# A message-passing megakernel on one core: the count build's part numbers are packed two to a 16-bit word

## The chip, the core and the metric

The kernel runs on one core of one Trainium2 chip. The metric is device time in microseconds (us) from the start to the end of one execution. The core has a matrix engine (TensorE: PE in the profile, with its weight loads as PEld and its instruction sequencer as PEldq), VectorE (DVE), ScalarE (ACT), GpSimd (POOL), SyncE (SP, which issues most DMAs) and 16 DMA engines.

## The reference

Four graph layers work in turn on 6250 nodes with 256 features each, over 100,000 edges, and each adds its result to the features. Cut to what matters here:

```python
edge_index = jnp.stack([src, dst])
h = jnp.maximum(_layernorm(x, axis=-1), 0.0)
x = x + _L0_gnn_ref(h, ..., edge_index)     # three rounds: agg = segment_sum(h[src], dst) / deg; then dense products
h = jnp.maximum(_layernorm(x, axis=-1), 0.0)
x = x + _L1_gnn_ref(h, ..., edge_index)     # attention over the edges
h = jnp.maximum(_layernorm(x, axis=-1), 0.0)
x = x + _L2_gnn_ref(h, ..., edge_index)     # two rounds: agg = segment_sum(x[col], row)
h = jnp.maximum(_layernorm(x, axis=-1), 0.0)
x = x + _L3_gnn_ref(h, src, dst, edge_type_2, ...)
```

The edges are sorted by `dst`, and low destinations get more edges than high ones. Layers 0 and 2 need sums over all edges of a node. The kernel turns these sums into products with a matrix of edge counts, `adj`, which it builds itself from `src` and `dst` at the start.

## The kernel before

The run has these stages: index preparation (0 to about 98 us), the **count build** (about 98 to 1004 us), then the passes that multiply node features with `adj` (layers 0 and 2, `L1352`), and between and behind them the gathers of layers 1 and 3. The change touches the count build alone.

The count build walks over the edges in 1592 steps (`MEETS`). One step is one chunk of 128 edges met with one block of 8 nodes. Steps are grouped in **turns** of 32 (`BUILD`). The first turn is written out, 47 turns run in a loop, and the last two are written out again; the last of them has 24 steps. A step does the following:

- VectorE makes a one-hot matrix of 128x392 for the step (`hot_columns`, L2309) into one of 16 buffers (`HOT`). For every 8 steps it makes one `hot_key` (L2304). It waits until TensorE is within 16 steps before it overwrites a buffer, in groups of 4 steps.
- TensorE multiplies the two into one of four PSUM banks (L1498). The bank is the step's **part number** modulo 4 (`own = z % RING`). Then it waits until the bank after that has been emptied (`evicted >= z`), and clears that bank with a tiny matmul (`cleared`, L1487). Steps with `s % 4 == 0` wait for VectorE as well (`hot`).
- ScalarE empties a finished bank into `staged` (L1723), and SyncE sends it to `adj` in DRAM (L732). There are 808 of these.

A part is a run of steps that add up in one bank. So the part number either stays the same from one step to the next or grows by one. The 1664 part numbers, one 32-bit word for each step (the last 72 are padding), lie in row 0 of the buffer `g_x` under the name `step_part`. A DMA puts them there before the build. TensorE's sequencer takes them into 16 registers (`zs`), 16 steps at a time (`NOW`), with one register load (L1493, TENSOR_LOAD in the profile) at steps 0 and 16 of a turn.

The part number decides the address of both matmuls of a step. So the sequencer computes two addresses in each step: a modulo, two multiplications and an addition for the first, the same with two more additions for the second. The compiler packs up to six such operations into one sequencer instruction (ISA in the listings below, FUSED_REGOPS in the profile). A step has two of them, and a step with a wait for `hot` a third, short one.

Between the steps, TensorE also carries the dense products of layer 0's first round, for one tile of nodes per turn: two transposes ahead of step 12 (`in_T`, L1193), products ahead of steps 29 and 30 (`in_P2`, L1212 and L1214), and products ahead of steps 1 and 2 of the turn after (`in_P3`, L1221). VectorE has a few instructions for these too.

No table sets the order here; it is the order of the code on each engine.

## Time and profile before

| | |
|---|---|
| median of 3 runs | 7671.14 us (7663.33 to 7676.74) |
| the profiled execution | 7667.53 us, of which 7665.8 us from the first to the last instruction |
| TensorE matmul busy, whole run | 82% |
| VectorE, ScalarE, GpSimd busy | 45%, 22%, 29% |
| count build, 100 to 1004 us | TensorE 725.4 us, VectorE 592.5 us, ScalarE 373.0 us busy of 904 |
| granted TensorE clock in the count build | 0.81 of full speed |

Times inside the profile count from the first instruction. A step's place in its turn is not written in the trace; it follows from the products between the steps (L1193 stands ahead of step 12, L1212 ahead of steps 29 and 30, L1221 ahead of steps 1 and 2).

### The profile page before, as it was taken

What the parts mean: (1) busy time and instruction counts of PE and PEld (TensorE: products, weight loads), DVE (VectorE), ACT (ScalarE), POOL (GpSimd) and SP (SyncE); (2) the same over time, 40 slices, a digit from 0 to 9 for tenths busy, and PEclk for the clock granted to TensorE, in tenths of its full rate; (3) what the DMA queues carried; (4) which work ended last, traced back from release to release, by engine and by line L of the source; (5) the groups of instructions that cost most, each with busy time, mean ns of one, the idle gap of its engine ahead of it and who ended that gap; (6) DMA issues with size and microseconds to landing.
All of it is one profiled execution on the core that took longest, in us unless ns stands there. A gap on an engine that the chain in (4) does not pass through costs nothing.

```text
span 7665.8 us, 108469 instructions
## 1 busy us (share of the span) xinstructions
PE 6321.0 (82%) x29032; PEld 4993.3 (65%) x29033; DVE 3412.8 (45%) x9453; ACT 1651.3 (22%) x4349; POOL 2239.8 (29%) x2541
## 2 busy tenths in 40 slices
PE   5877799999999999766676765999999966777677
PEld 3555477778887777655555554777787755555555
DVE  7766666661111222355555566122233324444443
ACT  1344410000000111111111113132233332222222
POOL 1000010001001111366666652000111116666664
PEclk8887799999999999878877887999999988878887
DMA  4566777788779777533333336988977753333332
GB/s 138 181 228 242 256 284 261 256 299 312 273 277 343 262 257 256 184 83 83 85 82 84 83 90 200 333 291 294 354 249 244 243 181 97 102 100 99 100 100 75
DMA packets 606869, 1525.79 MB, mean 199 GB/s; under 512 B 72808, under 2 KB 248915, under 8 KB 606612
## 3 DMA queue, kind: packets, MB, share of 16 engines
q1 hardware_dynamic: 472803, 1129.19, 41.8%
q0 software_dynamic: 133824, 393.46, 17.0%
q8 instruction: 143, 2.34, 0.1%
q14 instruction: 99, 0.80, 0.0%
HBM read 1206.47 MB, written 316.80 MB: 199 GB/s over the span
## 4 chain that ended last, share of the span: by engine, by line
PE 59%; DVE 11%; another core or an unknown queue 11%; issue 8%; DMA 6%; DVEq 2%; ACT 2%; SPq 1%; POOL 0%; ACTq 0%; POOLq 0%
PE psum L1352 33%; PE psum L1498 4%; PE psum L1198 4%; PE psum L1646 3%; PE psum L1618 2%; PE psum L1549 2%; DMA slab<-adj 2%; DVE hot_j L2309 2%; DVE acc L2547 2%; DMA g_own<-own_dram 2%; PE psum L1630 1%; PE psum L1537 1%; PE psum L1193 1%; PE psum L1286 1%
## 5 line engine op out<-in xcount | busy, mean ns | idle before, releaser
L1352 PE MATMUL psum<-X,slab 128*128 128x512 f32 x12495 | 3111.2, 402 | 74.9 <-DMA slab<-adj 41.3
L1352 PEld LDWEIGHTS psum<-X,slab 128*128 128x128 f32 x12495 | 2347.7, 191 | 608.5 <-DVE g_x L2374 89.7
L2547 DVE TENSOR_TENSOR acc<-acc,psum 128x264 f32 (+1 forms) x1660 | 702.8, 423 | 1068.8 <-PE psum L1646 353.0
L1498 PE MATMUL psum<-hot_j,hot_key 128*128 128x392 bf16 x1592 | 570.9, 431 | 164.2 <-DVE hot_j L2309 109.4
L1012 POOL DMA_DIRECT2D table<-s_tab x147 | 80.4, 547 | 1910.8 <-DVE s_tab L2065 1910.8
L1537 PE MATMUL psum<-node_tabs,onehot_t 128*128 x1660 | 274.7, 305 | 378.3 <-ACT onehot_t L1822 348.2
L1537 PEld LDWEIGHTS psum<-node_tabs,onehot_t 128*128 128x128 f32 x1660 | 274.0, 248 | 420.6 <-issue 414.3
L1102 POOL DMA_INDIRECT ring<-gat_table,idx_slot x420 | 415.7, 990 | 261.2 <-ACT idx_slot L1817 138.1
L1102 POOL DMA_INDIRECT ring<-rel_table,idx_slot x420 | 412.6, 982 | 250.2 <-ACT idx_slot L1817 137.7
L1723 ACT CAST staged<-psum 128x392 fp32r<-128x392 f32 x808 | 373.0, 489 | 522.3 <-PE psum L1498 497.0
L1498 PEld LDWEIGHTS psum<-hot_j,hot_key 128*128 128x128 bf16 x1592 | 235.7, 148 | 321.7 <-issue 236.2
L2309 DVE TENSOR_SCALAR hot_j<-iota_j,node_tabs 128x392 bf16<-128x392 bf16 x1592 | 411.2, 318 | 73.7 <-PE psum L1498 73.6
L2353 DVE TENSOR_TENSOR node_tabs<-node_tabs,slab 128x896 f32<-128x896 f32 x343 | 374.5, 1092 | 139.2 <-DMA slab<-adj 129.1
L1618 PEld LDWEIGHTS psum<-hT,wbuf 128*128 128x128 f32 x2064 | 383.5, 234 | 48.4 <-ACT hT L1974 2.6
L2065 DVE TENSOR_TENSOR s_tab<-psum,s_tab 128x256 fp32r<-128x256 f32 x196 | 83.1, 424 | 724.3 <-ACT s_tab L1690 724.3
L1618 PE MATMUL psum<-hT,wbuf 128*128 128x128 f32 x2064 | 375.0, 315 | 1.4 <-ACT hT L1974 1.4
L1685 ACT COPY s_hT<-psum 128x256 f32<-128x256 f32 x273 | 101.7, 373 | 1189.5 <-PE psum L1193 1189.5
L1198 PE MATMUL psum<-wbuf,s_hT 128*128 128x256 f32 (+1 forms) x1484 | 336.9, 363 | 0.0
L1487 PE MATMUL psum<-node_tabs 128*128 128x2 bf16 x1593 | 292.7, 184 | 14.2 <-ACT staged L1723 14.0
L1198 PEld LDWEIGHTS psum<-wbuf,s_hT 128*128 128x128 f32 x1484 | 274.9, 190 | 44.4
L1549 PE MATMUL psum<-ring,onehot 128*128 128x264 f32 x840 | 288.9, 481 | 16.7 <-DVE ring L2567 16.7
L1646 PE MATMUL psum<-ring,onehot 128*128 128x256 f32 x840 | 274.0, 420 | 20.6 <-DMA ring<-rel_table,idx_slot 20.3
(426 smaller groups left out, 8124.2 us busy)
## 6 DMA issues: line engine op xcount, KB each, us to landing
slab<-adj SPq DMA_DIRECT2D x383, 1344.0 KB, 6.7
slab<-adj SPq DMA_DIRECT2D x313, 896.0 KB, 6.2
adj<-staged SPq DMA_DIRECT2D x808, 196.0 KB, 1.9
X<-table SPq DMA_DIRECT2D x32, 1792.0 KB, 13.4
table<-s_tab POOLq DMA_DIRECT2D x196, 256.0 KB, 3.5
g_own<-own_dram POOLq DMA_DIRECT2D x35, 896.0 KB, 8.1
own_dram<-s_out POOLq DMA_DIRECT2D x196, 128.0 KB, 5.1
acc<-zero_rows SPq DMA_DIRECT2D x2, 6600.0 KB, 27.4
```

The source lines that it names most:

```text
L1102: nc.gpsimd.indirect_dma_start(out=to, out_offset=None, in_=tab, in_offset=bass.IndirectOffsetOnAxis(ap=idx_slot[:, r * HALF + u:r * HALF ...
L1198: last = nc.tensor.matmul(ps[:, 0:n], s_hT[:, q, :], w(q), start=(q == 0), stop=(q == Q - 1))
L1352: last = nc.tensor.matmul(sums_of(j), slab[:, slab_at(c), u, j * P:(j + 1) * P], X[:, x_at(p, d), :], start=(d == 0), stop=(d == KT - 1))
L1498: nc.tensor.matmul(psum[:, bass.ds(own, 1), 0:J].rearrange("p o j -> p (o j)"), hot_key[:, s % KEYS // AT_ONCE, :, s % AT_ONCE], hot_j[:, ...
L1537: last = nc.tensor.matmul(ps_log[:, v, :], onehot_t[:, v, :], dst_tab[:, bass.ds(tiles[v], 1), :].rearrange("p t h -> p (t h)"), start=Tru ...
L1549: nc.tensor.matmul(psum[:, v, 0:GW], onehot[:, r * HALF + v, :], homes[r][:, v, :], start=True, stop=True).then_inc(sem("mm"), 1)
L1618: last = nc.tensor.matmul(psum[:, bank, b * P:(b + 1) * P], wbuf[:, q, at:at + P], hT[:, q, :], start=(q == 0), stop=(q == Q - 1))
L1646: nc.tensor.matmul(psum[:, u % GB, 0:D], onehot[:, u, :], homes[r][:, v, 0:D], start=True, stop=True).then_inc(sem("mm"), 1)
L1723: nc.scalar.copy(staged[:, r, :], psum[:, (r + 1) % RING, 0:J]).then_inc(sem("evicted"), 1)
L2309: V.tensor_scalar(hot_j[:, s % HOT, :], iota_j[:], edge_now[:, s:s + 1], None, op0=ALU.is_equal).then_inc(sem("hot"), 1)
L2353: V.tensor_tensor(slab_sum, slab_sum, of[u], ALU.add).then_inc(sem("slab_summed" if u == SIZES[c] - 1 else "slab_partly"), 1)
L2547: V.tensor_tensor(a, a, psum[:, bank, 0:w], ALU.add).then_inc(sem("summed"), 1)
```

## The change

The part numbers of steps 2k and 2k+1 are added, and the sum is kept as one 16-bit word in a new row `pair_part` of 832 words. VectorE makes the row with one instruction on one partition, just before the build starts. TensorE loads 16 such words once per turn, at step 0, and takes a part number out of a sum with an addition (odd steps) and a floor division by two. The two numbers of a pair are equal or differ by one, so that is exact. TensorE now waits for `pair_part` instead of `step_part` before the build.

```diff
+    PAIRS = SB2 * P // 2
...
+                pair_part = sb("pair_part", [1, PAIRS], I16, scope=late)
...
             def build(t, steps):
                 for s in range(steps):
                     beside(in_stages, t, s)
-                    if s % NOW == 0:
-                        pe.load(zs, step_part[0:1, bass.ds(t * BUILD + s, NOW)])
-                    z = pe.snap(zs[s % NOW], min_val=1, max_val=LEAD + ENDED)
+                    if s == 0:
+                        pe.load(zs, pair_part[0:1, bass.ds(t * NOW, NOW)])
+                    if s % 2 == 0:
+                        both = pe.snap(zs[s // 2])
+                    z = pe.snap((both + s % 2) // 2, min_val=1, max_val=LEAD + ENDED)
                     if s % 4 == 0:
                         pe.wait_ge(*ev("hot", t * BUILD + (s + 4)))
...
-            pe.wait_ge(*ev("step_part", 16))
+            pe.wait_ge(*ev("pair_part", 1))
...
             dve.wait_ge(*ev("step_part", 16))
             dve.wait_ge(*ev("parts_stored", 16 * SB2))
+            of_pair = step_part.rearrange("p (n two) -> p n two", two=2)
+            V.tensor_tensor(pair_part, of_pair[:, :, 0], of_pair[:, :, 1], ALU.add).then_inc(sem("pair_part"), 1)
             V.tensor_copy(iota_k[:], iota_row[:])
```

On TensorE, around step 16 of a turn, the instructions stand like this before. L1494 and L1498 ISA are the address arithmetic ahead of a step's matmul, L1487 ISA that ahead of the clearing matmul:

```order
L1494 ISA
L1498 MATMUL psum<-hot_j,hot_key 128x392
L1487 ISA [waits evicted]
L1487 MATMUL psum<-node_tabs 128x2
L1493 TENSOR_LOAD g_x
L1498 ISA [waits hot]
L1498 MATMUL psum<-hot_j,hot_key 128x392
L1487 ISA [waits evicted]
L1487 MATMUL psum<-node_tabs 128x2
```

After, at the same place (the lines have moved by three to five):

```order
L1503 ISA
L1503 MATMUL psum<-hot_j,hot_key 128x392
L1490 ISA [waits evicted]
L1490 MATMUL psum<-node_tabs 128x2
L1503 ISA [waits hot]
L1503 MATMUL psum<-hot_j,hot_key 128x392
L1490 ISA [waits evicted]
L1490 MATMUL psum<-node_tabs 128x2
```

The load ahead of step 16 is gone, the one ahead of step 0 stays, and the number of arithmetic instructions per step is the same. Inside, the first arithmetic instruction of a step has one operation more: five become six (copy or add, divide, modulo, two multiplications, addition), and in a step with a wait for `hot` four become five.

On VectorE, just before the build, before:

```order
L2247 TENSOR_SCALAR tile_base<-tile_f 128x7 [waits dve_once]
L2331 CAST node_tabs<-iota_row 128x128 [waits table_moves,rec_stored,parts_stored,act_made,dve_once]
L2332 CAST iota_keys<-iota_row 128x1024
L2300 COPY node_tabs<-edge_at 128x16
L2081 TENSOR_SCALAR s_hT<-psum 128x256 [waits tile_P3,tile_T]
```

After:

```order
L2252 TENSOR_SCALAR tile_base<-tile_f 128x7 [waits dve_once]
L2337 TENSOR_TENSOR pair_part<-g_x 1x832 [waits table_moves,rec_stored,parts_stored,act_made,dve_once]
L2338 CAST node_tabs<-iota_row 128x128
L2339 CAST iota_keys<-iota_row 128x1024
L2305 COPY node_tabs<-edge_at 128x16
L2086 TENSOR_SCALAR s_hT<-psum 128x256 [waits tile_P3,tile_T]
```

One instruction is added ahead of all that VectorE does for the first step.

## Rows read from the trace of the kernel before

**Rows 1.** Build: busy us (count) of PE, PEld, DVE, ACT, POOL; granted clock, DMA.
```profile
100.00:1004.00 904.00, 725.40 (x3766) 467.80 (x3765) 592.46 (x2124) 373.03 (x808) 62.28 (x108) 0.81 0.59 213
```
**Rows 2.** Who waited for whom, 100 to 1004 us: total us, times, longest.
```profile
ACT staged L1723 <- PE psum L1498: 497.0, 506, 16.7
...
DVE hot_key L2304 <- PE psum L1498: 229.2, 116, 7.6
PE psum L1498 <- DVE hot_j L2309: 109.4, 65, 3.1
DVE hot_j L2309 <- PE psum L1498: 73.6, 48, 4.6
```
**Rows 3.** Matmuls around step 16 of one turn: start, us, [idle before].
```profile
464.92 0.39 PE L1498 MATMUL psum<-hot_j,hot_key 128*128 128x392 bf16 x1 [2.58 <-DVE hot_j L2309]
...
466.01 0.38 PE L1498 MATMUL psum<-hot_j,hot_key 128*128 128x392 bf16 x1
...
466.47 0.54 PE L1498 MATMUL psum<-hot_j,hot_key 128*128 128x392 bf16 x1
...
468.00 0.55 PE L1498 MATMUL psum<-hot_j,hot_key 128*128 128x392 bf16 x1
```
**Rows 4.** Weight loads of steps 15 and 16 in the same turn.
```profile
461.94 0.14 PEld L1498 LDWEIGHTS psum<-hot_j,hot_key 128*128 128x128 bf16 x1
...
464.92 0.14 PEld L1498 LDWEIGHTS psum<-hot_j,hot_key 128*128 128x128 bf16 x1 [2.70 <-issue]
```
**Rows 5.** Granted clock (PEclk) in the two stretches of rows 3.
```profile
464.90:466.30 1.40, 1.38 (x8) 0.95 (x8) 0.00 (x0) 0.71 (x2) 0.00 (x0) 1.00 0.42 158
466.40:469.70 3.30, 3.23 (x17) 2.21 (x17) 2.95 (x11) 1.70 (x5) 0.00 (x0) 0.50 0.61 227
```
**Rows 6.** L1493's register loads: ns min/median/max; all, then four single ones.
```profile
L1493 PEldq TENSOR_LOAD <-g_x x100: 1102/1840/3278, 98.4 to 999.5; - x100
...
L1493 PEldq TENSOR_LOAD <-g_x x1: 1120/1120/1120, 106.2 to 106.2; - x1
...
L1493 PEldq TENSOR_LOAD <-g_x x1: 2351/2351/2351, 462.3 to 462.3; - x1
...
L1493 PEldq TENSOR_LOAD <-g_x x1: 1617/1617/1617, 471.5 to 471.5; - x1
...
L1493 PEldq TENSOR_LOAD <-g_x x1: 1104/1104/1104, 999.5 to 999.5; - x1
```
**Rows 7.** The first matmul behind the load at step 0 at 471.5, with its idle time.
```profile
473.42 0.39 PE L1498 MATMUL psum<-hot_j,hot_key 128*128 128x392 bf16 x1 [1.01 <-DVE hot_j L2309]
```
**Rows 8.** Sequencer arithmetic of the steps: ns min/median/max.
```profile
L1494 PEldq FUSED_REGOPS  x1570: 47/94/108, 100.2 to 1003.6; - x197
...
L1498 PEldq FUSED_REGOPS  x398: 96/98/108, 99.8 to 1002.3; - x199
...
L1487 PEldq FUSED_REGOPS  x1592: 98/100/124, 100.0 to 1003.7; - x199
```
**Rows 9.** Sequencer arithmetic with a division (layer 1's L1537).
```profile
L1537 PEldq FUSED_REGOPS  x830: 98/137/161, 3187.4 to 4540.2; - x166
...
L1537 PEldq FUSED_REGOPS  x5: 107/137/149, 3850.3 to 3851.2; - x5
```
**Rows 10.** Loads of one word: 16-bit (L641) and 32-bit (L602).
```profile
L641 PEldq TENSOR_LOAD <-left_row x1: 309/309/309, 7621.2 to 7621.2; - x1
...
L602 PEldq TENSOR_LOAD <-half_row x44: 303/336/985, 3185.3 to 4528.5; - x44
```
**Rows 11.** A VectorE sum on one partition.
```profile
L2124 DVE TENSOR_TENSOR bound_row<-last_is,chunk_row x1: 961/961/961, 8.4 to 8.4; 1x782 f32<-1x782 int32 x1
```
**Rows 12.** What starts at the end of the build.
```profile
1004.13 2.78 PE L1352 MATMUL psum<-X,slab 128*128 128x512 f32 x8
...
1004.31 1.09 DVE L2347 TENSOR_TENSOR node_tabs<-slab 128x896 f32<-128x896 f32 x1 [6.39 <-PE psum L1498]
1004.55 1.73 POOL L1002 DMA_INDIRECT X<-table,idx_more  x1 [21.09 <-PE psum L1498]
```

More of the change, by code:

```diff
@@ L87, in build @@
     assert BTURNS == T + 1 and SB2 * P - MEETS + ENDED + MORE < ELSEWHERE
+    PAIRS = SB2 * P // 2
+    assert MEETS % 2 == 0 and BTURNS * NOW <= PAIRS
     KT = PARTS * DG // P
@@ L505, in build @@
                              ("cuts", 1), ("bound_read", 1), ("cuts_read", 1), ("z_rows", 1), ("parts_out", 1), ("marks", 1), ("x_ve", 1), ("more_rows", 1),
-                             ("b_self", 1), ("rows2_f", 2), ("x_rstd", 1), ("chunk_i", 1), ("edge_f", 2), ("turn_row", 1), ("w_att", 2 * Q),
+                             ("b_self", 1), ("rows2_f", 2), ("x_rstd", 1), ("chunk_i", 1), ("pair_part", 1), ("edge_f", 2), ("turn_row", 1), ("w_att", 2 * Q),
                              ("amax", 1), ("gdiag", 1), ("dst_tab", 1), ("zs_clamped", 1), ("bn_ve", 1), ("bn_shift", 1),
```

## The prediction

> **What bounds the kernel now.** The change touches only the count build, so I read that stretch first. By its busy times [rows 1] TensorE has 725 us of 904 and VectorE 592, so neither is full. The view of who waited for whom decides between them [rows 2]. VectorE waited for TensorE's L1498 for 229.2 + 73.6 = 303 us, which with its 592 us of work fills its 904 us. ScalarE waited for TensorE for 497 us. Both run behind TensorE. TensorE's own waits are small, and the largest is put down to VectorE's `hot_j`, 109.4 us. That name is wrong for most of it: in the turn of [rows 3] the idle 2.58 us stands exactly ahead of step 16, where the weight loads show a hole of 2.70 us with "issue" as its end [rows 4], and a register load of 2.35 us fills that hole [the one at 462.3, rows 6]. TensorE's sequencer is loading part numbers, and nothing else can be issued meanwhile.
>
> The second question is what paces a step when there is no load. If it were the array, a step would take longer at half clock. The turn of [rows 3] shows both levels of the clock back to back [rows 5]: the four steps from 464.92 to 466.47 run at full clock (2.4 GHz) and take 1.55 us; the next four, to 468.00, run at 0.50 (1.2 GHz) and take 1.53. So the array doesn't set the pace at either level. The sequencer's two arithmetic instructions do, of 94 to 98 and 100 ns [rows 8], with the issue of two weight loads and matmuls between them. **Each nanosecond added to that arithmetic lies on the path, and each taken from the loads comes off it.** At the build's end the next stage starts at once on TensorE, VectorE and GpSimd [rows 12], two of which had waited for L1498, so the whole rest moves with that end.
>
> **The load that goes.** There are 100 loads of 16 words, 1102 to 3278 ns [rows 6]: 50 at step 0 and 50 at step 16. Those at step 16, picked out by their place, sum to 115.7 us, a mean of 2.31 (the first, at 106.2, took 1120 ns, and the last, at 999.5, took 1104; they are the two shortest). One costs a little more than its own length. In the turn of [rows 4], step 16's weight load comes 2.98 us after step 15's; an ordinary step of the kind that waits for `hot` comes 0.46 after the one before (466.01 to 466.47, [rows 3]). That is 2.52 us lost, against 2.35 of the load itself: some 0.16 more, for the address arithmetic and the gaps. So **-(115.7 + 50 x 0.16) = -124 us**.
>
> The Trainium skill, "Runtime: NRT & Kernel Launch", section "Instruction fetch mechanics", puts a register load at about 200 ns per register, even in bulk. By it 16 registers take 3.2 us and the 50 loads 160 us, and the sum below would be 36 us better. The trace has that only as its longest load, so I don't use it.
>
> **The load that stays.** It now reads 16-bit words. No row shows 16 such words at once. A single 16-bit word took 309 ns, a single 32-bit word 303 at the least and 336 in the median [rows 10], so I take the width as free: 0. Below, if two words came in one access, the load at step 0 would halve. The 50 of them sum to 75.0 us, a mean of 1.5 (the one at 471.5 took 1617 ns, [rows 6]), and the build would win up to 50 x 0.75 = 37 us, since TensorE sits idle behind the one at 471.5 for 1.01 us [rows 7]. Above, 16-bit words could cost 10% more, the distance of L602's median from its minimum: 7 us.
>
> **The arithmetic that comes.** Each of the 1592 steps gets one more operation, a floor division by 2. The nearest rows are layer 1's L1537, where four of five instructions have a division and a modulo among six operations and the fifth has the modulo alone [rows 9]: 107 ns without the division, 137 in the median and 149 at the most within one group; 98 and 161 over all. Against the 94 ns of a step's instruction now [rows 8], 137 is +43; against the 98 of a step with a wait I take 135, +37. So 1194 x 43 + 398 x 37 = 66 us. The lower end is 137 - 107 = 30 ns or 48 us; the upper is 161 - 98 = 63 ns or 100 us. I stay near the median, as part numbers are small (at most some 800). Some of it is hidden: around steps 30, 31 and 1 the sequencer is held up by layer 0's products (L1212, L1214, L1221) and has time. That is three steps in 32: 6 us. **+60 us**.
>
> The second arithmetic instruction of a step (L1487) stays as it is, as does the number of instructions, so no gap between instructions is added.
>
> **Before the build.** VectorE's sum over 1x832 stands ahead of everything that the first step needs. A sum over 1x782 took 961 ns [rows 11]. Nothing covers it: **+1 us**. TensorE's changed wait ends with that instruction, long before `hot`, which it awaited anyway.
>
> **Moved waits.** What is late next once the stall at step 16 is gone? VectorE is 16 steps ahead at best and gets its lead back in TensorE's stalls. Its work is 592 us for 1592 steps, or 11.9 us a turn, and a turn is now 18.1 us long and then some 16.8. So it still has 5 us to spare per turn, and I put its new wait at 0. ScalarE spares more [rows 1, 2].
>
> **Sum:** -124 + 60 + 1 = -63 us. Against the profiled execution of 7667.5 us that is 7604.5; it lies 3.6 below the median of the runs, so the forecast for the median is 7671.1 - 63 = **7608 us**.
>
> **Rivals.**
>
> *Two words per access* (7608 - 37 = 7571 us). It speaks for it that the loaded bytes halve; against it, that one word costs the same at either width [rows 10]. 8%. A part of the same size could come from the clock. It stands at half right behind the stall at step 16 [rows 5], and without the stall layer 0's products at steps 29 and 30 may run at full clock; that is at most some 10 us, and in the range.
>
> *The division is dear* (7642 us). If it costs the 63 ns of the upper end in each step, 100 us are added, less 6 hidden: -124 + 94 + 1 = -29. For it: L1537's 149 to 161. Against it: these divide words much larger than ours. 13%.
>
> *VectorE takes over* (7640 us). With the stall gone VectorE's bunched work (`hot_key` and three to four instructions for layer 0 within 8 steps) makes TensorE wait for `hot` once a turn. Half of the gain would go: -32. For it: VectorE loses the stall in which it catches up. Against it: its 303 us of waiting. 10%.
>
> *The end of the build doesn't matter* (7671 us, no change). If the first pass waited for DMAs whose time doesn't depend on the build, the gain would be lost there. Against it [rows 12]: the engines start within half a microsecond of the last step, and GpSimd had been waiting 21 us for it. 4%.
>
> *Slower* (7722 us). One mechanism: the sequencer divides in a loop whose length goes with the quotient's bits, and a small divisor makes it long. It decides from 124/1592 = 78 ns per step. At 110 ns it adds 175 us against 124: +51. The divisors of L1537 are 64 and more, so division by 2 is not shown by any row; but its numbers are larger, and its longest instruction is 63 ns above its shortest, all told. 4%.
>
> *That the loads are not halved* is excluded by the listing: one load is left per turn, and it has 16 registers as before.
>
> **How the numbers follow.** The forecast has 61%, and the rivals 8, 13, 10, 4 and 4%. A measurement of this kernel can tell about 0.2% (15 us) from no change, so faster means below 7656. The forecast and the first three rivals lie there; I take 3% off them for values beyond their middle. Faster 0.89, same 0.07, slower 0.04. The range reaches to the first rival and past the next two: 7568 to 7652. It leaves out the last two and the tails, some 14%.
>
> **What would show it.** The register loads (now on L1496) should be 50, of 1.1 to 2 us each, all ahead of step 0. The median of the first arithmetic instruction of a step should be 130 to 145 ns. Four steps in a row should take about 1.70 us instead of 1.53 to 1.55, at either clock, and the idle time ahead of step 16 should be gone. The build should end near 1004 - 63 = 941 us, and everything behind it should be as long as before. I am wrong if the arithmetic shows 160 ns or more, if the 50 loads change their length by over a third, if TensorE's waits for `hot_j` don't shrink from 109 us to 30 or less, or if the stretch behind the build gives back what the build gains.

## The result, and the profile after

The changed kernel takes **7815.65 us** (median of 4 runs, 7802.06 to 7820.66), against 7667.24 of before (4 runs, 7658.87 to 7676.74) on the same chip. The ratio is 1.019, with a 95% interval of 1.0172 to 1.0209. The forecast was 7608, between 7568 and 7652. So the change costs 148 us where 63 were to be won.

The profiled execution of the changed kernel has a span of 7800.4 us, that of before 7665.8: +134.6. The build ends where TensorE's first pass begins. That is at 1138.48 us, against 1004.13 before [rows 12]:

```profile
1138.48 2.78 PE L1355 MATMUL psum<-X,slab 128*128 128x512 f32 x11
...
1138.72 1.73 POOL L1005 DMA_INDIRECT X<-table,idx_more  x1 [23.74 <-PE psum L1503]
```

So it ends 134.3 us later, and everything behind it is as long as before. The whole loss lies in the build. Its line of busy times (columns as in [rows 1]) and its waits (as in [rows 2]):

```profile
103.00:1138.00 1035.00, 798.44 (x3762) 477.02 (x3762) 586.77 (x2115) 373.66 (x808) 62.15 (x108) 0.79 0.52 186
```
```profile
PE psum L1503 <- issue: 180.5, 49, 5.7
...
PE psum L1503 <- DVE hot_j L2314: 4.0, 3, 1.9
...
ACT staged L1728 <- PE psum L1503: 619.5, 492, 20.4
...
DVE hot_key L2309 <- PE psum L1503: 348.5, 90, 11.6
```

VectorE's and ScalarE's work has not grown, and both wait longer for TensorE than before. TensorE is busy for 798 us where it was for 725, with as many matmuls; the clock explains that below. TensorE's idle time put down to `hot_j` has gone from 109.4 to 4.0 us, as forecast. In its place stand 49 idle times that end with "issue", 180.5 us in all and up to 5.7 us each. The sequencer's instructions tell what it did in them (ns min/median/max, first and last start):

```profile
L1496 PEldq TENSOR_LOAD <-pair_part x50: 3784/4576/6179, 99.2 to 1122.9; - x50
...
L1503 PEldq FUSED_REGOPS  x1194: 132/141/162, 103.3 to 1137.9; - x199
...
L1490 PEldq FUSED_REGOPS  x1592: 98/100/118, 103.5 to 1138.1; - x199
```

The arithmetic with the division has a median of 141 ns; 137 was forecast. The second instruction of a step stays at 100. But the **50 loads that stay take 4.58 us each** where 1.5 was forecast: 230.2 us in all (my sum over the 50 records) against the 75.0 that the same 50 took before. The 50 dropped at step 16 had taken 115.7. Half as many loads, each of half the bytes, cost 39.5 us more than all 100 did.

One turn shows what such a load does behind itself (start, us, [idle before]); below it are three stretches with the granted clock, the third figure from the end:

```profile
465.34 0.36 PE L1503 MATMUL psum<-hot_j,hot_key 128*128 128x392 bf16 x1
469.58 0.54 PE L1503 MATMUL psum<-hot_j,hot_key 128*128 128x392 bf16 x1 [3.87 <-issue]
469.99 1.20 PE L1224 MATMUL psum<-wbuf,s_hT 128*128 128x256 f32 x2
```
```profile
469.30:470.90 1.60, 1.32 (x4) 0.96 (x5) 0.00 (x0) 0.00 (x0) 0.00 (x0) 0.50 0.00 0
470.90:475.00 4.10, 4.10 (x20) 2.32 (x19) 1.58 (x5) 1.70 (x4) 0.00 (x0) 0.55 0.18 65
475.00:478.00 3.00, 2.82 (x19) 1.87 (x17) 3.00 (x12) 2.03 (x5) 1.08 (x2) 1.00 0.81 300
```

TensorE stands still for 3.87 us ahead of step 0, and then runs at half clock (1.2 GHz) just where layer 0's products L1224 come. These are float matmuls that keep the array busy: in the second stretch, which holds steps 1 to 9, it is busy for all 4.10 us. So here the array sets the pace and the sequencer runs ahead of it. In the median over the turns, step 2's clearing matmul starts 2.1 us behind its sequencer instruction, against 0.85 before (from the records). From 475.00 us on the clock is full again. Over the build the mean of these products goes from 474 to 701 ns (last two figures ahead of the idle time: sum in us, mean in ns), first before, then after:

```profile
L1221 PE MATMUL psum<-wbuf,s_hT 128*128 128x256 f32 x194 | 75.3, 474 | 0.0
```
```profile
L1224 PE MATMUL psum<-wbuf,s_hT 128*128 128x256 f32 x196 | 117.1, 701 | 0.0
```

VectorE's sum of the pairs took 1.01 us (forecast 1).

**The table to which I come back.** The time from one step's second sequencer instruction (L1487 before, L1490 after) to the next one's, worked out from the records and summed over the 50 turns, by the step's place in its turn, in us. Halved, pair32 and so on are the experiments below. The last column is how many turns of 50 were at half clock at step 6. Each row is one profiled execution. Probe turned out to be the same program as base, and the two differ by 7.7 us in the sum and by up to 3.9 in a column, so I don't read smaller differences.

| kernel | 0 | 1-4 | 5-9 | 10-15 | 16 | 17-18 | 19-31 | sum | half at 6 |
|---|---|---|---|---|---|---|---|---|---|
| before | 124.1 | 84.0 | 112.6 | 127.1 | 146.9 | 36.8 | 272.3 | 903.7 | 10 |
| after | 279.8 | 92.5 | 144.8 | 141.5 | 25.1 | 40.5 | 310.4 | 1034.6 | 46 |
| base | 122.5 | 85.3 | 115.3 | 126.9 | 148.2 | 36.7 | 274.7 | 909.6 | 11 |
| probe | 123.2 | 84.8 | 111.4 | 126.8 | 146.4 | 36.7 | 272.7 | 901.9 | 10 |
| halved | 122.1 | 92.6 | 124.8 | 139.1 | 143.4 | 40.7 | 290.4 | 953.2 | 14 |
| pair32 | 124.4 | 95.8 | 135.1 | 139.0 | 25.1 | 40.4 | 312.2 | 872.0 | 19 |
| load32 | 185.9 | 83.8 | 136.8 | 130.1 | 23.7 | 36.9 | 298.8 | 896.1 | 42 |
| load32at12 | 41.5 | 97.7 | 113.1 | 314.3 | 23.1 | 36.7 | 270.9 | 897.2 | 5 |
| load16at8 | 41.5 | 146.1 | 208.1 | 125.0 | 23.8 | 37.6 | 361.9 | 944.1 | 21 |
| pair32at8 | 43.1 | 110.8 | 205.1 | 137.0 | 25.5 | 40.9 | 298.8 | 861.3 | 12 |
| load4 | 70.8 | 162.4 | 175.5 | 156.4 | 63.5 | 36.6 | 349.3 | 1014.6 | 42 |

### The profile page after: what moved, and what is told of

It reads as the page before. It is cut to its first block, busy times and chain, and to the rows that moved or that the text cites. A ratio compares the mean times of both kernels' runs of the same rounds, so it can differ in the third digit from the quotient of the medians.

```text
span 7800.4 us, 108373 instructions
## 1 busy us (share of the span) xinstructions
PE 6397.5 (82%) x29032; PEld 5003.0 (64%) x29033; DVE 3407.3 (44%) x9454; ACT 1651.4 (21%) x4349; POOL 2236.6 (29%) x2541
## 4 chain that ended last, share of the span: by engine, by line
PE 58%; DVE 12%; another core or an unknown queue 11%; issue 9%; DMA 6%; DVEq 2%; ACT 2%; SPq 1%; POOL 0%; ACTq 0%; POOLq 0%
PE psum L1355 32%; PE psum L1503 4%; PE psum L1201 4%; PE psum L1651 3%; PE psum L1554 3%; PE psum L1623 2%; DMA slab<-adj 2%; DVE hot_j L2314 2%; DVE acc L2554 2%; PE psum L1635 2%; DMA g_own<-own_dram 1%; PE psum L1542 1%; PE psum L1224 1%; PE psum L1196 1%
## 5 line engine op out<-in xcount | busy, mean ns | idle before, releaser
L1355 PEld LDWEIGHTS psum<-X,slab 128*128 128x128 f32 x12495 | 2345.1, 190 | 610.0 <-DVE g_x L2381 92.6
L1503 PE MATMUL psum<-hot_j,hot_key 128*128 128x392 bf16 x1592 | 600.2, 420 | 215.3 <-issue 180.7
L1015 POOL DMA_DIRECT2D table<-s_tab x147 | 80.3, 546 | 1903.9 <-DVE s_tab L2070 1903.9
L1105 POOL DMA_INDIRECT ring<-gat_table,idx_slot x420 | 416.0, 990 | 254.9 <-issue 124.4
L1623 PEld LDWEIGHTS psum<-hT,wbuf 128*128 128x128 f32 x2064 | 380.7, 232 | 47.6 <-ACT hT L1979 2.6
L1490 PE MATMUL psum<-node_tabs 128*128 128x2 bf16 x1593 | 285.0, 179 | 22.6 <-ACT staged L1728 22.1
L975 POOL DMA_DIRECT2D table<-s_tab x49 | 27.3, 556 | 962.6 <-DVE s_tab L2070 962.6
```

What stands on the lines that cost most here:

```text
L1105: nc.gpsimd.indirect_dma_start(out=to, out_offset=None, in_=tab, in_offset=bass.IndirectOffsetOnAxis(ap=idx_slot[:, r * HALF + u:r * HALF ...
L1355: last = nc.tensor.matmul(sums_of(j), slab[:, slab_at(c), u, j * P:(j + 1) * P], X[:, x_at(p, d), :], start=(d == 0), stop=(d == KT - 1))
L1490: nc.tensor.matmul(bank_ap, iota_k[:], iota_k[:, 0:2], start=True, stop=True, skip_group_check=True)
L1503: nc.tensor.matmul(psum[:, bass.ds(own, 1), 0:J].rearrange("p o j -> p (o j)"), hot_key[:, s % KEYS // AT_ONCE, :, s % AT_ONCE], hot_j[:, ...
L1623: last = nc.tensor.matmul(psum[:, bank, b * P:(b + 1) * P], wbuf[:, q, at:at + P], hT[:, q, :], start=(q == 0), stop=(q == Q - 1))
```

## The experiments

They ran in five groups, each beside runs of before on its own chip. Before took 7180.21, 7663.48, 7618.84, 7186.94 and 7179.76 us there, so only the distance from before within a group counts. All kernels take a part number through a maximum with 0 in place of a copy (in ScalarE's loop too); `base` is before with that alone.

### Which part costs: the load, its place or the division (first group)

**base**, the yardstick:

```diff
-                    z = pe.snap(zs[s % NOW], min_val=1, max_val=LEAD + ENDED)
+                    z = at_least_0(pe, zs[s % NOW], min_val=1, max_val=LEAD + ENDED)
```

> The kernel before, with the copy of each part number into a fresh register written as max(number, 0) instead of min(number, number), on TensorE and on ScalarE; the number of operations is the same. It is the yardstick of the runs beside it. Every theory: 7667 us, within 0.2%; the 100 loads 1.1 to 3.3 us as before, a step's first arithmetic instruction 94 ns.

7185.94 us, ratio 1.0007 (0.9998 to 1.0016).

**pair32**: the changed kernel with its sums in 32-bit words (in `g_x`'s row, over `step_part`):

```diff
+                pair_row = step_part[:, 0:PAIRS]
...
+            V.tensor_copy(pair_row, pair_part).then_inc(sem("pair_part"), 1)
...
-                        pe.load(zs, pair_part[0:1, bass.ds(t * NOW, NOW)])
+                        pe.load(zs, pair_row[0:1, bass.ds(t * NOW, NOW)])
```

> The changed kernel, but the sums of two part numbers are kept as 32-bit words, in the place in g_x where the part numbers lay (VectorE makes the 16-bit row first, then copies it over, about 1 us more). Theory A (a 16-bit word costs a fetch of its own, about 0.29 us each, while 32-bit words cost 0.07 to 0.15): the 50 loads fall from 4.6 to about 1.5 us each and the time to about 7667 - 124 + 70 + 2 = 7615 us. Theory B (the place of the new row makes its load slow, whatever the width): the same, 7615. Theory C (the load at step 0 is long because VectorE no longer gets its lead back at step 16 and is at work on the same memory): the loads stay near 4.6 us and the time near 7815.

7152.49 us, ratio 0.9959 (0.9945 to 0.9973): 28 us under before.

**pair16gx**: pair32, but the row in `g_x` holds 16-bit words, `pair_row = step_part.bitcast(I16)[:, 0:PAIRS]`. Nothing else differs.

> As the run with 32-bit sums, with the same instructions and the row in the same place in g_x, but the words are 16 bits wide. Theory A (width): loads 4.6 us, time 7815. Theory B (place): loads 1.5 us, time 7615. Theory C (moment): loads 4.6 us, 7815, and then the 32-bit run must show the same.

7323.93 us, ratio 1.0202 (1.0189 to 1.0216). The load rows of pair32, then of pair16gx:

```profile
L1508 PEldq TENSOR_LOAD <-g_x x50: 1102/1377/2936, 90.9 to 952.5; - x50
```
```profile
L1508 PEldq TENSOR_LOAD <-g_x x50: 3787/4571/6269, 91.3 to 1116.0; - x50
```

Same place, same moment, same instructions: the word's width alone makes 3.2 us per load in the median, and 171 us of the time. The loss of the changed kernel is that of its 16-bit loads.

**halved**: before with every part number doubled by VectorE and divided by 2 by the sequencer, all 100 loads kept.

```diff
-                    z = pe.snap(zs[s % NOW], min_val=1, max_val=LEAD + ENDED)
+                    z = pe.snap(at_least_0(pe, zs[s % NOW], min_val=0, max_val=2047) // 2, min_val=1, max_val=LEAD + ENDED)
...
+            V.tensor_tensor(step_part, step_part, step_part, ALU.add).then_inc(sem("pair_part"), 1)
```

> The kernel before with its 100 loads of 16 32-bit words; the numbers are stored doubled and each step halves its own with a floor division. It prices the division alone. The profile of the changed kernel shows a step's first instruction at 141 ns instead of 94 (+47) and four steps at 1.70 instead of 1.55 us (+0.04 per step): 1592 x 0.045 = 72 us, less what is hidden at steps 30 and 31: 7667 + 68 + 1 = 7736 us. If the division were hidden at half clock or behind VectorE: under 7700.

7247.07 us, ratio 1.0092 (1.0077 to 1.0108): 61 us above base in the medians, 49 in the two profiled executions (base's was the slowest of its eleven). The 60 us for the division held.

### Is it the word, the sign or the burst (second and third group)

**pairu16** has the changed kernel's row as unsigned words (`mybir.dt.uint16` for `I16`).

> The changed kernel with its row of sums as unsigned 16-bit words in place of signed ones; nothing else differs. If the price is of the width (H1), the 50 loads keep their median of 4.5 to 4.6 us and the time is the changed kernel's: before + 2.0%, within 0.3%. If it is of the sign (H2: each word must be extended with its sign), the loads fall to 1.1 to 1.9 us and the time to before - 0.4%, as pair32.

7804.00 us, ratio 1.0194 (1.0178 to 1.0209), loads 3788/4563/6340 ns. The sign costs nothing.

**pair16in8** loads the sixteen words in two parts:

```diff
-                    if s == 0:
-                        pe.load(zs, pair_part[0:1, bass.ds(t * NOW, NOW)])
+                    if s % NOW == 0:
+                        pe.load(zs[s // 2:s // 2 + NOW // 2], pair_part[0:1, bass.ds(t * NOW + s // 2, NOW // 2)])
```

> The changed kernel, but its sixteen 16-bit words per turn are loaded as eight at step 0 and eight at step 16. If the dear 16-bit load costs by the word (G1: 4576 ns in the median for 16 is 286 a word, and a single 16-bit word took 309 in before), each of the 100 loads takes 2.2 to 2.5 us, their sum stays near 230 us, and the time is the changed kernel's within 0.3%: before + 2.0%. If a load of 16-bit words has a large fixed part (G2, say over 2 us), 8 words take 3.3 us or more, the sum grows by 100 us or more and the time is before + 3.4% or more. If it is the length of the burst that makes it dear (G3: eight words as cheap as 32-bit ones), they take 0.8 to 1.3 us each, and the time falls to about before - 0.2%.

7830.29 us, ratio 1.0226 (1.021 to 1.0241), between G1 and G2. The shortest load of eight took 1917 ns, half of the shortest of sixteen (3784): the price is by the word. The median of 2.85 us is above half of 4.58, because the load at step 16 stands in a costlier place (a mean of 3.37 us there, 2.46 at step 0); before shows that too (2.31 and 1.50).

**probe** was to time single loads ahead of the first step, with values that nothing used:

> Base with a probe ahead of the first step, where TensorE waits for VectorE: 13 register loads, four times over, whose values are not used. 1, 2, 4, 8 and 16 words of 32 bits; the same of 16 bits (from the same row); 16 words of 16 bits at every second place; 16 bytes; 16 words of 32 bits at every second place. By J1 (a narrow word is an access of its own of 250 to 300 ns, 32-bit words go in a burst): 16-bit words 0.3, 0.6, 1.2, 2.3, 4.6 us, 32-bit ones 0.3, 0.35, 0.5, 0.76, 1.1; 16 bytes 4.6 or more; the 32-bit words at every second place between 1.1 and 4.6. By J2 (the dear part is of the moment, not of the width: the array or the queues are busy at step 0): 16-bit loads of 16 words take under 2 us here. The sum of the probe is 50 to 100 us, which delays the first step by 40 to 100 us, as it starts after the last wait but one of TensorE.

7671.19 us (one run), and its trace holds none of the 52 loads: what nothing uses is not in the program. It is another run of base.

**probe2** uses each load's last register:

```diff
+            for _ in range(4):
+                pe.load(zs[0:1], step_part[0:1, 0:1])
+                pe.reg_alu(seen, zs[0], seen, ALU.max)
...
+                pe.load(zs[0:16], halves[0:1, 0:16])
+                pe.reg_alu(seen, zs[15], seen, ALU.max)
```

> The probe again: in the first one the values of its loads were not used, and its trace holds none of them. Now each load's last register goes into a maximum that the first weight load's address uses (its value is 0 at run time). Expected as before: by J1 (a narrow word is an access of its own) 1, 2, 4, 8, 16 words of 16 bits take 0.3, 0.6, 1.2, 2.3, 4.6 us and of 32 bits 0.3, 0.35, 0.5, 0.76, 1.1; 16 bytes 4.6 or more. The 100 loads of eight 16-bit words in pair16in8 took 2.87 us in the median (1.92 to 5.16), so a fixed part of 1.2 us with 0.21 us a word (J3) is possible too: then 1 word takes 1.4, which L652's single word of 0.31 speaks against; or what is in the way is the traffic of the moment (J2), then 16 words of 16 bits take under 2.5 us here.

7704.89 us (one run). The trace, with nothing else going on at TensorE. Lines 1524 to 1532 are 1, 2, 4, 8 and 16 words of 32 bits; 1534 to 1542 are 1, 2, 4, 8 and 16 of 16 bits; 1544 is 16 of 16 bits at every second place, 1546 is 16 bytes, 1548 is 16 words of 32 bits at every second place:

```profile
L1524 PEldq TENSOR_LOAD <-g_x x4: 308/314/486, 97.2 to 169.2; - x4
...
L1526 PEldq TENSOR_LOAD <-g_x x4: 546/547/549, 97.9 to 169.7; - x4
...
L1528 PEldq TENSOR_LOAD <-g_x x4: 339/339/347, 98.6 to 170.4; - x4
...
L1530 PEldq TENSOR_LOAD <-g_x x4: 592/596/596, 99.1 to 170.9; - x4
...
L1532 PEldq TENSOR_LOAD <-g_x x4: 1100/1103/1106, 99.9 to 171.7; - x4
...
L1534 PEldq TENSOR_LOAD <-g_x x4: 296/298/301, 101.1 to 172.9; - x4
...
L1536 PEldq TENSOR_LOAD <-g_x x4: 522/530/532, 101.6 to 173.4; - x4
...
L1538 PEldq TENSOR_LOAD <-g_x x4: 986/986/986, 102.3 to 174.1; - x4
...
L1540 PEldq TENSOR_LOAD <-g_x x4: 1918/1918/1919, 103.4 to 175.2; - x4
...
L1542 PEldq TENSOR_LOAD <-g_x x4: 3786/3786/3786, 105.5 to 177.3; - x4
...
L1544 PEldq TENSOR_LOAD <-g_x x4: 3783/3786/3787, 109.4 to 181.2; - x4
...
L1546 PEldq TENSOR_LOAD <-g_x x4: 3794/3798/3806, 113.4 to 185.2; - x4
...
L1548 PEldq TENSOR_LOAD <-g_x x4: 3801/3802/3813, 117.3 to 189.1; - x4
```

A 16-bit word costs some 233 ns each, from the first to the last ((3786 - 298) / 15). 32-bit words cost the same where they don't come in fours: two take 547, longer than four (339). **Four 32-bit words together cost as much as one** and a little: (1103 - 339) / 3 = 255 ns per group of four. Bytes and strided words go one by one.

**load32at10** was meant for another question (below), and showed a third condition. It loads 32 words per turn, at step 10:

```diff
+            LOAD_AT = 10
...
-                    if s % NOW == 0:
-                        pe.load(zs, step_part[0:1, bass.ds(t * BUILD + s, NOW)])
-                    z = at_least_0(pe, zs[s % NOW], min_val=1, max_val=LEAD + ENDED)
+                    if s == LOAD_AT:
+                        pe.load(zs, step_part[0:1, bass.ds(t * BUILD + LOAD_AT, BUILD)])
+                    z = at_least_0(pe, zs[(s - LOAD_AT) % BUILD], min_val=1, max_val=LEAD + ENDED)
...
+            pe.load(zs[BUILD - LOAD_AT:BUILD], step_part[0:1, 0:LOAD_AT])
```

> load32 with its one register load of 32 words per turn moved from step 0 to step 10 (the first ten words are loaded ahead of the loop). Same instructions otherwise. load32 won 124 us at step 16, lost 63 at step 0, and lost 47 in the other 30 steps, although these have the same instructions: 21 of it in steps 5 to 9 and 24 in steps 19 to 31. M1 (clock): the longer load at step 0 leaves TensorE at half clock in steps 1 to 8 in 35 to 44 turns of 50 (12 or 13 in base), just where layer 0's long float products run, while the load at step 16 had put the half clock where only short steps run. Then the load at step 10 puts it into steps 11 to 20, steps 5 to 9 fall from 137 to about 115 us, the build ends 20 us earlier and the time is before - 25 us (some 0.3%). M2 (VectorE or the write-outs are the next limit, wherever the load stands): steps 5 to 9 and 19 to 31 keep their sum, or the loss moves behind the load, and the time is before - 0 to - 8 us, as load32.

7882.07 us, ratio 1.0352 (1.0338 to 1.0366): 263 us over before, far outside both.

**pair32at10** is pair32 with its load at step 10:

> pair32 (sums of two in 32-bit words, one load of 16 words per turn, division in each step) with the load at step 10 in place of 0; the first five words are loaded ahead of the loop. pair32 was before - 28 us (ratio 0.9959). M1 (clock): in pair32 20 to 23 turns of 50 were at half clock in steps 1 to 6, against 12 in base, so about half of load32's loss, 10 us, comes back, and the load no longer adds to the gap of the loop's end: before - 40 us, 0.9945. M2: as pair32, before - 28 us, 0.996.

7741.78 us, ratio 1.0172 (1.0158 to 1.0186): 123 us over before, far outside both again. The load rows of load32at10, pair32at10, and load32at12 from the next group:

```profile
L1506 PEldq TENSOR_LOAD <-g_x x50: 7733/9214/10045, 102.2 to 1251.0; - x50
```
```profile
L1510 PEldq TENSOR_LOAD <-g_x x50: 3807/5418/6776, 103.7 to 1117.9; - x50
```
```profile
L1506 PEldq TENSOR_LOAD <-g_x x50: 2136/3558/4553, 96.3 to 982.1; - x50
```

The shortest are 242 ns a word for 32 words that begin 40 bytes behind a turn's start, 238 for 16 that begin at 20 bytes, and 67 for 32 that begin at 48. Starts at 0, 48 and (in pair32at8 below) 16 bytes were fast, starts at 20 and 40 slow. These five fit one rule: the start must lie at a multiple of 16 bytes, or no four go together.

### Where the rest of the expected gain went (second, fourth and fifth group)

pair32 removes the load at step 16 without making the other dearer, and wins 33 us over base, though step 16 falls by 123.1 us in the table and the division costs 61 or less. So some more comes back elsewhere.

**load32** drops step 16's load without any division: one load of 32 words at step 0, 8 groups of four.

```diff
-                    if s % NOW == 0:
-                        pe.load(zs, step_part[0:1, bass.ds(t * BUILD + s, NOW)])
+                    if s == 0:
+                        pe.load(zs, step_part[0:1, bass.ds(t * BUILD, BUILD)])
```

> Before with one register load of 32 32-bit words per turn in place of two of 16; no pairs, no division, the arithmetic of a step as before (in its max form). Taken from the job before this one: the 100 loads of 16 words sum to 191.7 us in base, the 50 at step 0 alone to 73.9 in pair32 (mean 1.48). If a load costs by the word (E1), the 50 loads sum to 180 to 190 us again and only the lost gaps are won: 5 to 10 us. If most of a 32-bit load is a fixed part (E2: the step from 8 words, 0.76 us, to 16, 1.10, is 43 ns a word), the 50 sum to 50 x (1.48 + 16 x 0.043) = 108 us, and 191.7 - 108 + 8 = 92 us come off the sequencer. What the build then gives back is the second question. In pair32 the steps other than 16 took 85 us more than in base, of which a division explains 49 by halved; some 36 us were new waits (for ScalarE's staged, for DMAs). F1: these waits come whenever the stall at step 16 goes; then load32 has them too, the gain is 92 - 36 = 55 us, and the time is before - 55. F2: they belong to the code with the pairs; then load32 gains about 90 us. A gain of under 15 us speaks for E1.

7654.27 us, ratio 0.9995 (0.9986 to 1.0004); loads 2129/2717/3485 ns. Step 16 gives 124.5 us, step 0 takes 63.4, and the other thirty steps, whose instructions are unchanged, take 47.6 more: 21.5 in steps 5 to 9 and 24.1 in 19 to 31. So F1's waits came with plain code too, and were larger than its 36 us. The time forecasts missed: I had a gain of 55 us or more under E2, and it is 9. I had also written that a gain under 15 us speaks for E1, and that sign pointed wrong: the loads took 139.1 us in all, between E2's 108 and E1's 180 to 190.

**load32at12** is load32at10 with `LOAD_AT = 12`.

> load32at10 with the load at step 12. In load32at10 the 50 loads of 32 words took 7.7 us at the least (9.2 in the median), in load32 2.1 (2.7): only the place of their first word differs, 40 bytes behind a multiple of 128 against 0. The second probe has 1, 2, 4, 8, 16 words of 32 bits at 315, 547, 339, 596, 1106 ns. N1: four 32-bit words that begin at a multiple of 16 bytes come in one access of some 255 ns, any other word is an access of its own of some 235. Step 12 begins at 48 bytes: the loads take 2.1 us at the least and 2.7 in the median, as in load32. N2: only a start at a multiple of 64 or 128 bytes is fast (or a load at this place in the turn is slow whatever its address): 7.7 us again, and before + 3.5%. If N1 holds, the run is also the trial of the clock that load32at10 was meant for. M1: steps 5 to 9 fall from load32's 137 us to about 115, before - 25 us. M2: they don't, before - 0 to - 8 us.

7173.95 us, ratio 0.9983 (0.9972 to 0.9994), 13 us under before. N1's shortest load held (2136 ns), its median of 2.7 us didn't (3.56). M1's mechanism held: steps 5 to 9 fall from 136.8 to 113.1, with 5 turns at half clock at step 6 against 42. Its size of 25 us didn't. Against that stand the load itself (beside step 12 its 50 take 178.5 us, not 139.1) and steps 1 to 4, 13.9 us longer. The products that follow step 0, in base, load32 and load32at12:

```profile
L1232 PE MATMUL psum<-wbuf,s_hT 128*128 128x256 f32 x193 | 76.8, 484 | 0.0
```
```profile
L1232 PE MATMUL psum<-wbuf,s_hT 128*128 128x256 f32 x196 | 103.4, 625 | 0.0
```
```profile
L1232 PE MATMUL psum<-wbuf,s_hT 128*128 128x256 f32 x194 | 69.8, 444 | 0.0
```

**load16at8** moves base's two loads to steps 8 and 24 (`if s % NOW == LOAD_AT`) and nothing else.

> Base with its two loads of 16 words per turn at steps 8 and 24 in place of 0 and 16; no pairs, no division. It asks what the place of a load alone is worth. Q1: a load at step 8 instead of 0 wins what it won in pair32at8 over pair32 (15 us), and the one at 24 costs what it cost at 16: before - 10 to - 15 us. Q2: the loads at step 24 end just ahead of layer 0's products at steps 29 and 30 and leave them at half clock, and the place wins nothing: before - 3 to + 15 us.

7222.12 us, ratio 1.0058 (1.0045 to 1.0072): 42 us over before, some 37 over base, which had lain 6 over before. I had the direction with Q2, not the size. The two stops are cheaper themselves (steps 0 and 16 fall by 205 us, steps 8 and 24, worked out in the same way, rise by 163), and 49 of 50 turns are at half clock at step 30, where base has 18. Steps 1 to 4 rise from 85.3 to 146.1 us: there the sequencer, ahead of the array, waits for the products to get through. Step 2's clearing matmul starts 2.7 us behind its sequencer instruction in the median, against 0.85 in base (from the records). Some 12 us of the rise come without the half clock: load32at12 has no load at step 0 either, 5 turns at half clock, and 97.7 us in these steps. L1223, the one at steps 29 and 30, has a mean of 666 ns (base 483):

```profile
L1223 PE MATMUL psum<-wbuf,s_hT 128*128 128x256 f32 x192 | 108.6, 666 | 0.0
```

So the same loads in another place cost some 37 us, most of it by the clock of what stands behind them.

The 24 us in steps 19 to 31 have another face. ScalarE's and TensorE's waits for the write-out of finished parts, over the build, in base, load32 and load32at12:

```profile
ACT staged L1734 <- DMA adj<-staged: 16.3, 8, 4.2
...
PE psum L1498 <- ACT staged L1734: 11.5, 18, 1.9
```
```profile
ACT staged L1734 <- DMA adj<-staged: 35.0, 12, 6.4
...
PE psum L1498 <- ACT staged L1734: 33.8, 34, 3.3
```
```profile
ACT staged L1737 <- DMA adj<-staged: 12.7, 6, 3.6
...
PE psum L1498 <- ACT staged L1737: 12.2, 22, 2.7
```

In a few stretches in which two steps of three end a part (13 or 14 write-outs in 20 steps; over the build it is one step of two), the eight `staged` buffers wait for their DMAs. In load32 these land up to 8.6 us after their issue, against 1.9 in the median. A stop of TensorE at steps 12 or 16 covers such a wait, and without the stop it shows. In the changed kernel ScalarE's wait for these DMAs is 28.0 us. Base has as many slow landings (over 3 us: 102 of 808, against 91 of 707 in load32, whose trace lacks the other landings); load32at10, which stops for 9.2 us in every turn, has 8 of 707, so they come with the pace of the steps. This is read from traces alone: no run changed the write-out, and why these DMAs are slow stays open.

**load4** has no long stop at all, a load of four words at every fourth step (`if s % 4 == 0: pe.load(zs, step_part[0:1, bass.ds(t * BUILD + s, 4)])`):

> Before with a load of four 32-bit words at every fourth step (8 loads a turn) in place of 16 words at every sixteenth. The same words in the same number of 16-byte accesses, but never more than one at a time. By N1 each load takes 339 ns when all is quiet, some 450 in the build (there 16 words take 1.84 us in the median against 1.10), 398 of them 180 us against base's 191. O1: a load costs its length and 0.16 us of gaps wherever it stands: 398 x 0.16 - 16 = 48 us more, before + 40 to + 50 us. O2: short stops are hidden where the array or a wait for the one-hots holds TensorE up anyway, and the half clock behind the long stop goes: before - 10 to - 30 us. By N2 (four words alone are not fast in the build) the loads take 0.9 us each and the time is before + 2 to 3%.

7290.98 us, ratio 1.0149 (1.0132 to 1.0166), 104 us over before; neither O1 nor O2. The loads are short, as N1 has it, but the build's clock is the lowest of all, and the products' mean is 699 ns:

```profile
L1504 PEldq TENSOR_LOAD <-g_x x398: 327/334/1257, 89.8 to 1103.5; - x199
```
```profile
95.00:1104.00 1009.00, 859.67 (x3749) 508.09 (x3746) 593.26 (x2113) 375.21 (x808) 62.05 (x108) 0.66 0.53 191
```

By the table, steps 4, 8, 12 and so on cost what O1 said (a load and its gap, some 0.6 us), about 40 us more than base's two long loads. The other 65 stand mostly in steps 1 to 7, behind products at half clock. Many small stops were worse for the clock than two long ones: base has 0.81 here.

**pair4** does the same to pair32, four words at every eighth step:

> pair32 (sums of two in 32-bit words, division in each step) with a load of four words at every eighth step in place of 16 at every 32nd. By N1 200 loads of some 0.45 us, 90 us against the 74 of pair32. O1: 150 more gaps of 0.16 us and 16 us of loads: pair32's - 28 becomes before + 12 us. O2: the loads hide beside layer 0's products and the waits for the one-hots: before - 35 to - 50 us, the fastest of all kernels here.

7205.85 us, ratio 1.0027 (1.0017 to 1.0037), 19 us over before, close to O1.

### The load at step 8, and fewer divisions (fourth and fifth group)

**pair32at8**: pair32at10 with `LOAD_AT = 8`, whose words begin at 16 bytes.

> pair32at10 with the load at step 8, so that its 16 words begin at the fourth word of a turn, a multiple of 16 bytes. N1: 50 loads of 1.1 us at the least and 1.4 to 1.8 in the median (5.4 at step 10, where they began 20 bytes behind a multiple of 64). N2: 3.8 us and more, before + 1.7%. With N1, M1 (the clock) gives before - 40 us, M2 as pair32 before - 28 us.

7144.30 us, ratio **0.9943** (0.9928 to 0.9958), 43 us under before; loads 1108/1407/1922 ns. N1 held. The size is M1's, but its interval touches that of pair32 (0.9945 to 0.9973), and the half clock at step 6 fell only from 19 turns to 12, so what the place is worth here is not shown.

**pairsub8** divides in even steps only:

```diff
-                    z = pe.snap((both + s % 2) // 2, min_val=1, max_val=LEAD + ENDED)
+                    z = pe.snap(both // 2, min_val=1, max_val=LEAD + ENDED) if s % 2 == 0 else at_least_0(pe, both - z, min_val=1, max_val=LEAD + ENDED)
```

> pair32at8, but only an even step divides: z0 = sum // 2, and the odd step takes z1 = sum - z0, a subtraction and a maximum in place of an addition and a division. halved cost 61 us over base for 1592 divisions; if each division is some 35 to 46 ns on the path (P1), half of them is 25 to 35 us: pair32at8's 0.9943 becomes 0.990 to 0.991, some 65 to 75 us under before. P2: with the divisions half gone the sequencer is no longer what paces an ordinary step (VectorE or ScalarE are), and the time stays within 8 us of pair32at8's.

7136.23 us, ratio 0.994 (0.9927 to 0.9954), 44 us under before and not told apart from pair32at8. P1's 65 to 75 us failed; P2's time, within 8 us of pair32at8, came true. The odd steps' arithmetic only falls from 143 to 117 ns (medians of the 796 records), since a subtraction and a maximum are not free. The odd steps stand on L1517 in pair32at8 and on L27 in pairsub8, each with others beside them; first pair32at8, then pairsub8:

```profile
L1517 PEldq FUSED_REGOPS  x1176: 132/141/147, 96.2 to 944.5; - x196
```
```profile
L27 PEldq FUSED_REGOPS  x1517: 42/117/146, 95.7 to 941.4; - x190
```

A plain odd step (13, 15, 17 or 19 of a turn) falls from 400 to 374 ns, so there the sequencer still sets the pace, and P2's reason for its time isn't shown. That would be 796 x 26 = 21 us; the build's sum falls from 861.3 to 850.9 in the traces, hardly more than base and probe differ, and the medians show 1 us. Where the rest went stays open; my price for a division taken out was too high.

## Why the prediction was wrong

- **The load that goes** (-124): held. Step 16 falls from 146.9 to 25.1 us, -121.8.
- **The load that stays** (0): **the step that failed**. It measured +155.2 in the loads and +155.7 in the table's step 0. I took the width as free because one 16-bit word costs what one 32-bit word costs [rows 10]. Probe2 shows the same (298 and 314 ns), and also that it says nothing of sixteen: 32-bit words go four at a time and 16-bit words don't. The bounds of -37 and +7 us came from the same single words, so the range had no room for it. The row that could have warned was in [rows 6]: 16 words in 1102 ns are 69 ns each, against 303 for one alone [rows 10], so a load of many has a discount, and I gave the new form the same one without a row for it.
- **The price per register**, which I left out: the Trainium skill, "Runtime: NRT & Kernel Launch", section "Instruction fetch mechanics", has about 200 ns per register even in bulk. For the loads of before that is too much, and there the measurement decides (69 ns per word in the shortest, 119 at the mean). For the loads of after it is about right: 16 x 200 is an estimate of 3.2 us, and the shortest took 3.78. I asked of it only whether it fits the loads that are there, not whether it fits the new ones. (With 160 us for the loads the prediction's sum would be 44 us better, not 36; I had left out the 8 us of gaps.)
- **The arithmetic** (+60): held. 141 ns against 137, four steps in a row take 1.72 us (the sum of the medians of their kinds) against 1.70, and halved costs 49 to 61 us.
- **Before the build** (+1): 1.01 us.
- **Moved waits** (0): wrong by some 48 us. Outside steps 0 and 16 the changed kernel is 97.0 us longer than before, and halved explains 48.8 of it (687.7 against base's 638.9). About 23 stand in steps 5 to 9, behind the half clock, and 22 in steps 19 to 31, where the write-outs of parts show. In pair32, without the dear loads, the same sum gives some 35. I asked only VectorE for spare time. The 4.0 us of `hot_j` here say little, for a turn takes 20.8 us and not my 16.8; pair32, at 17.5, shows that it was right: 26.7 us are put down to `hot_j`, and 30 of the 31 idle times overlap a register load (my count). I had not asked what clock the products beside step 0 would get, nor what the stop at step 16 had been covering.
- **Behind the build**: held, 134.6 against 134.3.

The table's sum: 155.7 - 121.8 + 97.0 = +130.9, and the first step's second instruction starts 3.5 us later, 2.7 of it by the length of its own load. Of my signs of being wrong, one came: the 50 loads changed their length by over a third (from 1.50 to 4.60 us at the mean). Without the width's price the change would have been worth 28 us (pair32), not 63: then the direction and the division were right, and the moved waits took half. Of the rivals, "two words per access" had the right question, whether words come in groups, and the wrong sign.

## What to carry to other kernels

A register load is cheap only in groups of four 32-bit words that begin at a multiple of 16 bytes (255 ns a group, 64 ns a word; starts at 0, 16, 20, 40 and 48 bytes were tried); narrow, strided or misplaced words cost some 235 ns each, so pack for fewer words and keep them 32 bits wide. A price measured on one element bounds nothing for sixteen: compare the per-element price at both counts before calling a format free. Where a sequencer's stop can't be avoided, put it where short latency-bound steps follow, not ahead of long float products: the same two loads moved by eight steps cost some 37 us.

## What the runs showed of the hardware

- Loads by the sequencer: 1, 2, 4, 8, 16 words of 32 bits take 314, 547, 339, 596 and 1103 ns; of 16 bits 298, 530, 986, 1918 and 3786.
- In the build the same load takes longer. At step 0 it is 1.2 times for sixteen 16-bit words (4.58 us in the median against 3.79) and 1.4 times for 32-bit ones (1.50 at the mean against 1.10), at step 16 2.1 times (2.31 at the mean against 1.10). The 16-bit load grows from some 4.0 us to some 5.0 over the build. What it shares with the DMAs or VectorE is open.
- With two loads a turn, of 1.5 and 2.3 us, the build's mean granted clock was 0.81 (base), with eight, 398 in all, of 0.33 us it was 0.66 (load4).
